# First cross-attention of a Perceiver block: the output product from rounded parts and rests, issued later in the next tile

## The chip, the cores and the metric

The kernel runs on one core of a Trainium2 chip. The metric is the device time of one execution in microseconds. TensorE multiplies, ScalarE and VectorE empty its results from PSUM and do the elementwise work, GpSimd (POOL) clips and does small powers, and the SP queue issues nearly all transfers. Each engine runs its own instruction stream in order; semaphores join the streams.

## The reference, cut to what matters

Six blocks follow one another (cross-attention, self-attention, mixture of experts, cross-attention, self-attention, feed-forward). The change lies in the first, for 16 batches of 64 latents and 256 context rows, width 256, 16 heads of 64 (INNER = 1024):

```python
lat = layernorm(latents, ln_l_w, ln_l_b)
ctx = layernorm(context, ln_c_w, ln_c_b)
q = (lat @ Wq)
k, v = jnp.split(ctx @ Wkv, 2, axis=-1)
attn = jnp.clip(jnp.einsum('bhnd,bhsd->bhns', q, k) * scale, -11.0, 11.0)
attn = jax.nn.softmax(attn, axis=-1)
out = jnp.einsum('bhns,bhsd->bhnd', attn, v)       # heads side by side: 1024 wide
return out @ Wo + bo                               # the output product
```

All is float32, and the result is added to x.

## The kernel before, in words

The stage works in 8 tiles t of 128 latents (two batches, 512 context rows). The key weights are folded into the queries (fill_A), so that scores are taken against the normalised context cT itself. Values (fill_v) and scores use pairs: an operand is rounded to fp32r (hi), the rest is subtracted (lo), and three one-pass products hi hi, hi lo, lo hi stand for one float32 product. The output product alone is a plain float32 one: 8 products of 128x128 by 128x256, which the profile shows as 16 matmul records of line 693.

TensorE's order in a tile t, written out by hand in pe_x0: v2, v3 and scores 0 to 3 in turn, then y(t-1), the output product of the tile before, then the transposes lat(t+1), then v4, scores 4, v5, scores 5, v6, scores 6, v7, values 0, scores 7, then q(t+1), A(t+1), values 1 and v0, v1 of the next tile. All these fills but the scores and values go through a ring of four PSUM banks; the list FILLS fixes the order, and each bank must have been emptied by ScalarE or VectorE before its next use.

Between two tiles the attention result and the normalised context are transposed by a way through DRAM: VectorE writes rows (att, cn), the SP queue stores and reloads them in blocks (turn_rows, turn_att_rows), and VectorE turns 32x32 blocks (turn_context, turn_att). In the last tile TensorE transposes instead (fill_T), in two halves, and two half products y and y2 (fill_y_half, line 701) lie among the first steps of the self-attention stage (pe_self, span 0).

VectorE's order in a tile t: norm(t+2) part 0, turn_context(t+1), turn_att(t-1) twice, v3, cT(t+1), cT_split(t+1), residual(t-1) with its row statistics, norm(t+2) part 1 (two statistics of line 315 and five aggregations of line 320), v5, norm part 2, v7, norm part 3, attend 0, q, A_lower and so on. The rstd for the norm comes from GpSimd (line 327). ScalarE's order: exponentials 0 and 1, v2, exponentials 2 and 3, cT(t+1) (line 754), lat(t+1), v4, exponentials 4 and 5, v6, and so on. cT_split rounds cT (line 899) and subtracts (cT_lo, line 901); it needs both halves of cT, ScalarE's and VectorE's.

Only in tiles with a successor is there a cT, only in those with two a norm. Behind the stage GpSimd adds a bias row to x (line 2111), and the self-attention stage's first steps on VectorE include maximum (lines 1961 to 1967) and rotate (line 1941). The weights w_sq[0] are read from line 1486 on, the expert weights from line 2311 on.

## Time and profile before

| | us |
|---|---|
| median of 3 runs | 1001.73 |
| lowest, highest | 998.05, 1005.35 |
| the profiled execution's own time | 1003.49 |
| its span, first to last instruction | 1001.8 |
| mean granted TensorE clock, of full speed | 0.981 |

The profile is of one execution. Its rows name a line, an engine, an operation, out<-in by the program's names, and shapes in partitions x elements; starts are in us from the span's beginning. A number in brackets behind a row is the engine's idle time before the instruction and what ended it. TensorE's matmuls are pipelined: their length is longer than the distance between their starts, and it is this distance that counts in a stream.

### The profile page before, as it was taken

To read this page: it belongs to the slowest core of one execution; us is meant where nothing else is said; L and a number is where in the kernel's file an instruction comes from. 1 tells how busy PE (TensorE), PEld (TensorE's weight loads), DVE (VectorE), ACT (ScalarE), POOL (GpSimd) and SP (SyncE) were. 2 spreads that over 40 slices of the span, in tenths; PEclk is the share of its full clock that TensorE was granted. 3 is DMA by queue.
4 is the path that set the end of the run, shared out by engine and by line. 5 is a ranking of instruction groups with operands and counts; after the bars stand their busy time and mean duration, and the time that the engine had idled before them with its cause. 6 is when DMAs were issued, how large, how long until landed. Compare 5 with 4: busy or idle time off the path is not lost.

```text
span 1001.8 us, 25859 instructions
## 1 busy us (share of the span) xinstructions
PE 949.6 (95%) x10657; PEld 815.0 (81%) x10657; DVE 613.0 (61%) x1448; ACT 446.1 (45%) x892; POOL 169.3 (17%) x357
## 2 busy tenths in 40 slices
PE   5899999999999989999879999997999999999998
PEld 5788888888888777887669999995888888877887
DVE  5655754654532655667798787776787763554242
ACT  3333332433332476654236666652435343673241
POOL 2312112113112213334320000013113000101000
PEclk9999999999999999999979999997999999999999
DMA  9443142131210292000049999952312002000000
GB/s 321 129 106 74 33 106 68 39 85 42 45 37 7 67 381 98 3 12 24 20 129 332 380 357 358 328 129 57 59 36 45 3 2 76 2 2 1 8 14 22
DMA packets 158611, 101.14 MB, mean 101 GB/s; under 512 B 102104, under 2 KB 148128, under 8 KB 157984
## 3 DMA queue, kind: packets, MB, share of 16 engines
q1 hardware_dynamic: 156960, 95.31, 32.0%
q0 software_dynamic: 1536, 4.20, 1.3%
q8 instruction: 85, 1.39, 0.6%
q14 instruction: 30, 0.25, 0.1%
HBM read 82.96 MB, written 16.52 MB: 99 GB/s over the span
## 4 chain that ended last, share of the span: by engine, by line
PE 82%; DVE 9%; ACT 5%; issue 2%; DMA 1%; POOL 0%; SPq 0%; DVEq 0%; ACTq 0%; POOLq 0%
PE ps L642 9%; PE ps L657 8%; PE ps L2367 8%; PE ps L2380 6%; PE ps L2703 6%; PE ps L674 3%; PE ps L1486 3%; PE ps L1195 3%; PE ps L1583 3%; PE ps L596 2%; PE ps L693 2%; PE ps L626 2%; PE ps L1525 2%; PE ps L1120 2%; PE ps L1130 2%
## 5 line engine op out<-in xcount | busy, mean ns | idle before, releaser
L2367 PE MATMUL ps<-moe_xT,ew 128*128 128x128 f32 x736 | 91.3, 278 | 2.2 <-issue 1.2
L2367 PEld LDWEIGHTS ps<-moe_xT,ew 128*128 128x128 f32 x736 | 87.6, 195 | 3.2 <-DVE moe_xT L2453 1.9
L785 ACT ACTIVATE x0pT<-ps 128x512 f32<-128x512 f32 x64 | 38.2, 598 | 111.1 <-PE ps L657 111.1
L1029 POOL TENSOR_SCALAR x0pT<-x0pT 128x512 f32<-128x512 f32 x64 | 40.6, 635 | 188.3 <-ACT x0pT L785 187.2
L2703 PE MATMUL ps<-f,ffw 128*128 128x512 f32 x256 | 60.7, 398 | 0.8 <-issue 0.6
L2703 PEld LDWEIGHTS ps<-f,ffw 128*128 128x128 f32 x256 | 48.9, 192 | 12.0 <-issue 0.9
L642 PE MATMUL ps<-x0wv_hi,x0cT_hi 128*128 128x512 f32 x128 | 53.6, 418 | 4.2 <-DVE x0A_lo L915 4.2
L2380 PE MATMUL ps<-ew_2hi,eh_hi 128*128 128x256 f32 x184 | 55.4, 301 | 1.7 <-DVE eh_lo L2506 1.3
L2316 DVE TENSOR_TENSOR ew_2lo<-ew,ew_2hi 128x1024 fp32r<-128x1024 f32 x46 | 55.9, 1216 | 0.0
L2563 POOL DMA_INDIRECT yg<-moe_out,slot x16 | 16.3, 1017 | 230.9 <-DMA moe_out<-moe_y 163.5
L915 DVE TENSOR_TENSOR x0A_lo<-ps,x0A_hi 128x512 fp32r<-128x512 f32 x64 | 39.8, 683 | 23.4 <-ACT x0A_hi L776 23.3
L657 PE MATMUL ps<-x0A_hi,x0cT_hi 128*128 128x512 f32 x128 | 51.5, 403 | 2.6 <-ACT x0pT L785 2.6
L921 DVE COPY x0v<-ps 128x512 f32<-128x512 f32 x32 | 22.0, 687 | 50.5 <-PE ps L642 50.5
L2380 PE MATMUL ps<-ew_2hi,eh_lo 128*128 128x256 f32 x184 | 51.7, 281 | 0.0
L2380 PE MATMUL ps<-ew_2lo,eh_hi 128*128 128x256 f32 x184 | 51.6, 281 | 0.0
L642 PE MATMUL ps<-x0wv_hi,x0cT_lo 128*128 128x512 f32 x128 | 50.9, 398 | 0.0
L642 PE MATMUL ps<-x0wv_lo,x0cT_hi 128*128 128x512 f32 x128 | 50.9, 397 | 0.0
L657 PE MATMUL ps<-x0A_lo,x0cT_hi 128*128 128x512 f32 x128 | 50.7, 396 | 0.0
L657 PE MATMUL ps<-x0A_hi,x0cT_lo 128*128 128x512 f32 x128 | 50.2, 392 | 0.0
L389 POOL TENSOR_TENSOR rn_tmp<-rn_cur,eps 128x1 f32<-128x1 f32 x48 | 13.2, 275 | 215.0 <-DVE rn_cur L383 214.3
L2311 ACT ACTIVATE ew_2hi<-ew 128x1024 fp32r<-128x1024 f32 x46 | 49.3, 1072 | 0.0
L2415 ACT ACTIVATE eh<-ps,b1x 128x128 f32<-128x128 f32 x120 | 34.3, 369 | 32.3 <-PE ps L2367 32.3
(336 smaller groups left out, 2416.6 us busy)
## 6 DMA issues: line engine op xcount, KB each, us to landing
ew<-L_ffn_W_dram SPq DMA_DIRECT2D x46, 1024.0 KB, 7.9
x0cin<-ctx_dram SPq DMA_DIRECT2D x8, 512.0 KB, 4.7
x1cin<-ctx_dram SPq DMA_DIRECT2D x64, 64.0 KB, 2.3
x0cn_rows<-x0cn SPq DMA_DIRECT2D x7, 512.0 KB, 2.8
x0cn_blocks<-x0cn_rows SPq DMA_DIRECT2D x56, 64.0 KB, 2.4
x0att_rows<-x0att SPq DMA_DIRECT2D x14, 256.0 KB, 2.5
x0att_blocks<-x0att_rows SPq DMA_DIRECT2D x56, 64.0 KB, 2.7
moe_out<-moe_y SPq DMA_DIRECT2D x23, 128.0 KB, 4.4
```

The costliest lines, as they stand in the source:

```text
L642: last = nc.tensor.matmul(dst, m[:, k, tok * P:tok * P + P], w[:, k, half * 512:half * 512 + 512], start=(k == 0 and n == 0), stop=(k == K ...
L657: last = nc.tensor.matmul(ps[:, S_BANK[u % 2], :], w[:, k, keys], m[:, k, b, pg, :, :, :].rearrange("p a j n -> p (a j n)"), start=(k == 0 ...
L674: last = nc.tensor.matmul(ps[64 * b:64 * b + 64, PV_BANK + par, j * VW:j * VW + VW], g.pT[:, 4 * pg + 2 * b + kt, at_p:at_p + N], g.v[:, 2 ...
L785: nc.scalar.activation(g.pT[:, u, :], ps[:, S_BANK[u % 2], :], ACT.Exp, scale=64.0 ** -0.5).then_inc(C0.exp, 1)
L915: nc.vector.tensor_tensor(g.A_lo[:, kc, :, pg, par, :, :].rearrange("p b j n -> p j b n"), bank_of(t, f"A{gr}{par}").rearrange("p (j b n) ...
L1029: nc.gpsimd.tensor_scalar(g.pT[:, u, :], g.pT[:, u, :], high, low, ALU.min, ALU.max).then_inc(C0.clip, 1)
L2311: nc.scalar.activation(ew2_hi[b % 2][:, sl, :], ew2[b % NW2][:, sl, :], ACT.Copy).then_inc(MO.w_hi, 1)
L2316: nc.vector.tensor_tensor(ew2_lo[b % NW2][:, sl, :], ew2[b % NW2][:, sl, :], ew2_hi[b % 2][:, sl, :].bitcast(F32), ALU.subtract).then_inc( ...
L2367: last = nc.tensor.matmul(ps[:, n % 3, j * BT:j * BT + BT], ew1[b % NW][:, i, f * P:f * P + P], xT[b % 2][:, i, :], start=(i == 0), stop=( ...
L2380: last = nc.tensor.matmul(ps[:, o_bank(b), 0:D], v[:, j * BT:j * BT + BT], w[:, f, :], start=(f == 0 and m == 0), stop=(f == FT - 1 and m ...
L2415: last = nc.scalar.activation(eh[n % 3][:, j * BT:j * BT + BT], ps[:, n % 3, j * BT:j * BT + BT], ACT.Gelu_apprx_tanh, bias=bias)
L2703: last = nc.tensor.matmul(ps[:, 2 + f % 4, :], w[:, k, f * P:f * P + P], src[part][:, k, :], start=(k == 0 and part == 0), stop=(k == ks - ...
```

## The change

The output product is taken as three one-pass products from rounded parts and rests, as the other products are. For this, in tile 0, ScalarE rounds Wo to wo_hi and VectorE subtracts wo_lo, in four pieces each; in tiles 1 to 7 ScalarE rounds attT(t-1) to attT_hi in two pieces behind cT(t+1), and VectorE subtracts attT_lo in two pieces behind norm(t+2) part 1. The product y(t-1) moves behind v5, ahead of scores 5; the residual moves behind v5 on VectorE. In the last tile each half is rounded by ScalarE and its rest taken by VectorE. attT_lo and wo_lo lie over attT and wo. wo_hi lies where w_sq[0] is, so these weights are loaded when the stage is done; attT_hi lies in half of padneg, which is cleared again by a memset on GpSimd then. Counts of semaphores follow (C0.turned, C0.attT, pool_setup), without other effect.

```diff
             attT = sb("x0attT", [P, 8, P])
...
             wo = sb("x0wo", [P, 8, D])
+            wo_lo = nc.alloc_sbuf_tensor_at("x0wo_lo", [P, 8, D], F32R, offset=wo_at)
+            wo_hi = nc.alloc_sbuf_tensor_at("x0wo_hi", [P, 8, D], F32R, offset=w_sq_at)
+            attT_hi = nc.alloc_sbuf_tensor_at("x0attT_hi", [P, 8, P], F32R, offset=padneg_at + B * S)
...
-            FILLS += [(("x0", t - 1), "y")] * (t > 0) + [(("x0", t + 1), "lat")] * nxt
-            FILLS += [(("x0", t), f"v{i}") for i in range(4, 8)]
+            FILLS += [(("x0", t + 1), "lat")] * nxt
+            FILLS += [(("x0", t), f"v{i}") for i in range(4, 6)] + [(("x0", t - 1), "y")] * (t > 0)
+            FILLS += [(("x0", t), f"v{i}") for i in range(6, 8)]
...
+            def out_products(t, what, ks):
+                for k in ks:
+                    for n, (m, w) in enumerate(((g.attT_hi, g.wo_hi), (g.attT_hi, g.wo_lo), (g.attT_lo, g.wo_hi))):
+                        last = nc.tensor.matmul(bank_of(t, what)[:, 0:D], m[:, k, :], w[:, k, :], start=(k == ks[0] and n == 0), stop=(k == ks[-1] and n == 2))
+                last.then_inc(C0.fill, 1)
...
                 if t == 0:
-                    pe.wait_ge(ld["x0o"], 16)
-                pe.wait_ge(C0.attT, 2 * t + 2)
+                    pe.wait_ge(C0.w_lo, KD + 4)
+                pe.wait_ge(C0.attT, 4 * t + 4)
...
-                for k in range(8):
-                    last = nc.tensor.matmul(bank_of(t, "y")[:, 0:D], g.attT[:, k, :], g.wo[:, k, :], start=(k == 0), stop=(k == 7))
-                last.then_inc(C0.fill, 1)
+                out_products(t, "y", range(8))
...
             def fill_y_half(t, what):
                 half = ("y", "y2").index(what)
                 wait_emptied(pe, t, f"T{half}")
...
-                for k in range(4):
-                    last = nc.tensor.matmul(bank_of(t, what)[:, 0:D], g.attT[:, 4 * half + k, :], g.wo[:, 4 * half + k, :], start=(k == 0), stop=(k == 3))
-                last.then_inc(C0.fill, 1)
+                out_products(t, what, range(4 * half, 4 * half + 4))
...
-                if t > 0:
-                    fill_y(t - 1)
                 if nxt:
                     fill_lat(t + 1)
                 for i in range(4, 8):
                     fill_v(t, i)
+                    if i == 5 and t > 0:
+                        fill_y(t - 1)
                     if i == 7:
                         values(t, 0)
                     scores(t, i)
...
-            def attT(t):
-                wait_filled(act, t, "T0")
-                nc.scalar.activation(g.attT[:, 0:4, :], bank_of(t, "T0"), ACT.Copy).then_inc(C0.by_act, 1)
+            def attT_upper(t):
+                act.wait_ge(C0.attT, 4 * t + 2)
+                if t > 0:
+                    wait_filled(act, t - 1, "y")
+                for pg in range(2):
+                    nc.scalar.activation(g.attT_hi[:, 4 * pg:4 * pg + 4, :], g.attT[:, 4 * pg:4 * pg + 4, :], ACT.Copy).then_inc(C0.attT_hi, 1)
+
+            def attT_upper_last(pg):
+                wait_filled(act, T - 1, f"T{pg}")
+                nc.scalar.activation(g.attT_hi[:, 4 * pg:4 * pg + 4, :], bank_of(T - 1, f"T{pg}").rearrange("p (c n) -> p c n", c=4), ACT.Copy).then_inc(C0.attT_hi, 1)
...
+            def wo_upper(i):
+                if i == 0:
+                    act.wait_ge(ld["x0o"], 16)
+                nc.scalar.activation(g.wo_hi[:, 2 * i:2 * i + 2, :], g.wo[:, 2 * i:2 * i + 2, :], ACT.Copy).then_inc(C0.w_hi, 1)
...
@@ -811,13 +833,22 @@
                 exp(t, 3)
                 if nxt:
                     cT(t + 1)
+                if t > 0:
+                    attT_upper(t - 1)
+                if nxt:
                     lat(t + 1)
                 v(t, 4)
                 exp(t, 4)
                 exp(t, 5)
+                if t == 0:
+                    wo_upper(0)
+                    wo_upper(1)
                 v(t, 6)
                 exp(t, 6)
                 exp(t, 7)
+                if t == 0:
+                    wo_upper(2)
+                    wo_upper(3)
                 if nxt:
                     q(t + 1)
                     A_upper(t + 1, 0)
...
-            def attT(t):
-                wait_filled(dve, t, "T1")
-                nc.vector.tensor_copy(g.attT[:, 4:8, :], bank_of(t, "T1")).then_inc(C0.by_dve, 1)
+            def attT_lower(t, pg):
+                dve.wait_ge(C0.attT_hi, 2 * t + pg + 1)
+                half = slice(4 * pg, 4 * pg + 4)
+                nc.vector.tensor_tensor(g.attT_lo[:, half, :], g.attT[:, half, :], g.attT_hi[:, half, :].bitcast(F32), ALU.subtract).then_inc(C0.attT, 1)
+
+            def attT_lower_last(pg):
+                dve.wait_ge(C0.attT_hi, 2 * T - 1 + pg)
+                half = slice(4 * pg, 4 * pg + 4)
+                nc.vector.tensor_tensor(g.attT_lo[:, half, :], bank_of(T - 1, f"T{pg}").rearrange("p (c n) -> p c n", c=4),
+                                        g.attT_hi[:, half, :].bitcast(F32), ALU.subtract).then_inc(C0.by_dve, 1)
+
+            def wo_lower(i):
+                dve.wait_ge(C0.w_hi, KD + i + 1)
+                nc.vector.tensor_tensor(g.wo_lo[:, 2 * i:2 * i + 2, :], g.wo[:, 2 * i:2 * i + 2, :], g.wo_hi[:, 2 * i:2 * i + 2, :].bitcast(F32), ALU.subtract).then_inc(C0.w_lo, 1)
...
                 if nxt:
                     cT(t + 1)
                     cT_split(t + 1)
+                if more:
+                    norm(t + 2, 1)
+                if t > 0:
+                    attT_lower(t - 1, 0)
+                    attT_lower(t - 1, 1)
+                v(t, 5)
                 if t > 0:
                     residual(t - 1)
-                if more:
-                    norm(t + 2, 1)
-                v(t, 5)
                 if more:
                     norm(t + 2, 2)
                 v(t, 7)
                 if more:
                     norm(t + 2, 3)
+                if t == 0:
+                    wo_lower(0)
+                    wo_lower(1)
                 attend(t, 0)
                 if nxt:
                     q(t + 1)
+                if t == 0:
+                    wo_lower(2)
+                    wo_lower(3)
+                if nxt:
                     A_lower(t + 1, 0)
                     A_lower(t + 1, 1)
                     attend(t, 1)
...
-                pe.wait_ge(ld["sq0"], 64)
...
+                if n == LEAD - 2:
+                    pe.wait_ge(ld["sq0"], 64)
...
                 hT(lo)
-                last(T - 1)
+                last(0)
                 lat(lo)
                 qkc(lo)
                 rope(lo)
+                last(1)
                 hT(lo + 1)
                 lat(lo + 1)
                 qkc(lo + 1)
                 hT(lo + 2)
...
                 x0_attend, x0_attT, x0_add_y, x0_residual = last
+                x0_attT(0)
                 rotate(lo)
                 x0_attend(T - 1, 1)
                 v(lo)
                 norm(lo + 1)
-                x0_attT(T - 1)
+                x0_attT(1)
                 norm(lo + 2)
                 x0_add_y(T - 1, "y")
                 maximum(lo)
...
-            for i, w in enumerate(("Wq", "Wk", "Wv", "Wo")):
-                whole(w_sq[0][:, :, i, :], weight("L0_ffn_" + w), ld["sq0"])
...
             sp.wait_ge(C0.x_done, T)
+            for i, w in enumerate(("Wq", "Wk", "Wv", "Wo")):
+                whole(w_sq[0][:, :, i, :], weight("L0_ffn_" + w), ld["sq0"])
             for i, w in enumerate("QKVO"):
                 whole(w_sq[1][:, :, i, :], weight("L1_attn_W_" + w), ld["sq1"])
-            sp.wait_ge(pool_setup, 8)
+            sp.wait_ge(pool_setup, 9)
...
             pool.wait_ge(C0.x_done, T)
+            nc.gpsimd.memset(padneg[:, B // 2:B, :], 0.0).then_inc(pool_setup, 1)
             nc.gpsimd.memset(b2[:, :], 0.0).then_inc(pool_setup, 1)
             nc.gpsimd.memset(minus1[:, :], -1.0).then_inc(pool_setup, 1)
             pool_self(pool, 0)
```

## Rows read from the trace of the kernel before

**Rows 1.** TensorE's waits, 0 to 480 us: who waited <- for whom, sum, times, longest.

```profile
PE ps L642 <- DVE x0A_lo L915: 4.2, 8, 0.6
```

**Rows 2.** Timeline of TensorE, tile 3: start, length, instruction.

```profile
153.72 3.62 PE L693 MATMUL ps<-x0wo,x0attT 128*128 128x256 f32 x16
...
157.18 0.38 PE L583 MATMUL ps<-cst,x0lat 128*128 128x128 f32 x2
...
161.58 0.39 PE L657 MATMUL ps<-x0A_hi,x0cT_hi 128*128 128x512 f32 x1
```

**Rows 3.** Timeline of TensorE, expert stage.

```profile
561.57 0.28 PE L2380 MATMUL ps<-ew_2hi,eh_lo 128*128 128x256 f32 x1
...
562.71 1.95 PE L2367 MATMUL ps<-moe_xT,ew 128*128 128x128 f32 x16
```

**Rows 4.** Timeline of VectorE, tile 3.

```profile
155.98 1.22 DVE L901 TENSOR_TENSOR x0cT_lo<-x0cT,x0cT_hi 128x1024 fp32r<-128x1024 f32 x1
...
160.03 0.45 DVE L320 BATCH_NORM_AGGREGATE ln_mv<-ln_st 128x2 f32<-128x6 f32 x5
161.78 0.69 DVE L921 COPY x0v<-ps 128x512 f32<-128x512 f32 x1 [1.30 <-PE ps L642]
```

**Rows 5.** Timeline of ScalarE, tile 3.

```profile
154.41 0.80 ACT L754 ACTIVATE x0cT<-x0cT,col 128x512 f32<-128x512 f32 x1
```

**Rows 6.** Timeline of VectorE, tile 0.

```profile
45.07 1.23 DVE L901 TENSOR_TENSOR x0cT_lo<-x0cT,x0cT_hi 128x1024 fp32r<-128x1024 f32 x1
...
47.46 0.66 DVE L921 COPY x0v<-ps 128x512 f32<-128x512 f32 x1
```

**Rows 7.** VectorE's subtractions: one line's instructions (ns min/median/max), and a timeline row.

```profile
L2506 DVE TENSOR_TENSOR eh_lo<-eh,eh_hi x46: 691/693/694, 517.2 to 665.4; 128x512 fp32r<-128x512 f32 x46
...
176.24 2.48 DVE L915 TENSOR_TENSOR x0A_lo<-ps,x0A_hi 128x512 fp32r<-128x512 f32 x4 [1.02 <-ACT x0A_hi L776]
```

**Rows 8.** Timeline of TensorE, a first matmul behind a wait.

```profile
105.14 0.50 PE L642 MATMUL ps<-x0wv_hi,x0cT_hi 128*128 128x512 f32 x1 [0.51 <-DVE x0A_lo L915]
```

**Rows 9.** Timelines of TensorE in tile 1 and of VectorE in tiles 1 and 6.

```profile
76.17 3.69 PE L693 MATMUL ps<-x0wo,x0attT 128*128 128x256 f32 x16 [0.20 <-issue]
...
78.14 1.22 DVE L901 TENSOR_TENSOR x0cT_lo<-x0cT,x0cT_hi 128x1024 fp32r<-128x1024 f32 x1
...
272.18 1.22 DVE L901 TENSOR_TENSOR x0cT_lo<-x0cT,x0cT_hi 128x1024 fp32r<-128x1024 f32 x1
```

**Rows 10.** Timeline of VectorE, behind the last product of the stage.

```profile
342.10 0.42 DVE L949 TENSOR_TENSOR x_res<-ps,x_res 128x256 f32<-128x256 f32 x1 [0.29 <-PE ps L701]
```

**Rows 11.** Timeline of VectorE, line 1967 in two places of the next stage.

```profile
346.64 0.65 DVE L1967 SCALAR_TENSOR_TENSOR sa_neg<-sa_max,sa_neg 128x16 bf16<-128x16 f32 x1
...
366.10 0.17 DVE L1967 SCALAR_TENSOR_TENSOR sa_neg<-sa_max,sa_neg 128x16 bf16<-128x16 f32 x1
```

**Rows 12.** Timeline of GpSimd, beside these two, and in tile 3.

```profile
160.84 1.18 POOL L327 TENSOR_TENSOR ln_rs<-ln_ve,neghalf 128x5 f32<-128x5 f32 x1
...
345.17 2.09 POOL L2111 TENSOR_TENSOR x_res<-x_res,rows 128x256 f32<-128x256 f32 x3
...
365.70 0.55 POOL L400 TENSOR_TENSOR rn_tmp<-rn_tmp,neghalf 128x1 f32<-128x1 f32 x1
```

**Rows 13.** TensorE by stretches of tile 0: us, busy (instructions), granted clock, DMA.

```profile
43.50:46.00 2.50, 0.00 (x0) 1.00 0.06 22
47.00:50.00 3.00, 3.00 (x8) 0.50 0.02 5
```

**Rows 14.** Instructions of three lines (ns min/median/max, first and last start us).

```profile
L1486 PE MATMUL ps<-sa_hT,w_sq x128: 275/275/377, 374.1 to 466.0; 128*128 128x128 f32 x128
...
L2311 ACT ACTIVATE ew_2hi<-ew x46: 1052/1072/1079, 373.3 to 664.8; 128x1024 fp32r<-128x1024 f32 x46
...
L2930 POOL MEMSET padneg<- x1: 3520/3520/3520, 1.6 to 1.6; 128x4096 bf16 x1
```

**Rows 15.** The page, part 6: a DMA issue, KB, us to landing.

```profile
ew<-L_ffn_W_dram SPq DMA_DIRECT2D x46, 1024.0 KB, 7.9
```

More of the change, by code:

```diff
@@ L91, in build @@
         maskTi = sb("maskTi", [P, B, 2], I32)
+        padneg_at = at[0]
         padneg = sb("padneg", [P, B, S], BF16)
@@ L173, in build @@
             att = sb("x0att", [P, 8, P])
+            attT_at = at[0]
             attT = sb("x0attT", [P, 8, P])
+            attT_lo = nc.alloc_sbuf_tensor_at("x0attT_lo", [P, 8, P], F32R, offset=attT_at)
             wq = sb("x0wq", [P, KD, INNER])
@@ L179, in build @@
             wv_hi = sb("x0wv_hi", [P, KD, INNER], F32R)
+            wo_at = at[0]
             wo = sb("x0wo", [P, 8, D])
+            wo_lo = nc.alloc_sbuf_tensor_at("x0wo_lo", [P, 8, D], F32R, offset=wo_at)
+            wo_hi = nc.alloc_sbuf_tensor_at("x0wo_hi", [P, 8, D], F32R, offset=w_sq_at)
+            attT_hi = nc.alloc_sbuf_tensor_at("x0attT_hi", [P, 8, P], F32R, offset=padneg_at + B * S)
             ln_st = sb("ln_st", [P, 5, 6])
@@ L484, in build @@
             attT = sem("c0_attT")
+            attT_hi = sem("c0_attT_hi")
             cT_act = sem("c0_cT_act")
-            cT_dve = sem("c0_cT_dve")
             cT_hi = sem("c0_cT_hi")
@@ L546, in build @@
         _more += [(("x1", t), k) for t in range(T) for k in ("q", "k1")]
-        RS = Ring([ps[:, i, :] for i in range(4)], FILLS, ("cT1", "q1", "K1", "K3", "v1", "v3", "v5", "v7", "T1", "rope", "k", "pv", "y", "y2", "router", "rank"),
+        RS = Ring([ps[:, i, :] for i in range(4)], FILLS, ("cT1", "q1", "K1", "K3", "v1", "v3", "v5", "v7", "T0", "T1", "rope", "k", "pv", "y", "y2", "router", "rank"),
                   SA.fill, SA.by_act, SA.by_dve, _more)
@@ L752, in cT @@
                 else:
-                    act.wait_ge(C0.turned, t)
+                    act.wait_ge(C0.turned, 2 * t - 1)
                 nc.scalar.activation(g.cT[:, 0, :], bank_of(t, "cT0") if t == 0 else g.cT[:, 0, :], ACT.Identity,
@@ L827, in act_x0 @@
                     A_upper(t + 1, 3)
-            return attT
+            return attT_upper_last
         def self_tables(dve):
@@ L887, in cT @@
                 else:
-                    dve.wait_ge(C0.turned, t)
+                    dve.wait_ge(C0.turned, 2 * t - 1)
                 nc.vector.tensor_scalar(g.cT[:, 1, :], bank_of(t, "cT1") if t == 0 else g.cT[:, 1, :], vec("ln_c_w", 1), vec("ln_c_b", 1),
-                                        ALU.mult, ALU.add).then_inc(C0.by_dve if t == 0 else C0.cT_dve, 1)
+                                        ALU.mult, ALU.add).then_inc(C0.by_dve if t == 0 else C0.turned, 1)
             def cT_split(t):
@@ L897, in cT_split @@
                     dve.wait_ge(C0.cT_act, t)
-                    dve.wait_ge(C0.cT_dve, t)
+                    dve.wait_ge(C0.turned, 2 * t)
                 nc.vector.tensor_copy(g.cT_hi[t % 2][:, :, :], g.cT[:, :, :]).then_inc(C0.cT_hi, 1)
@@ L1020, in dve_x0 @@
                     self_tables(dve)
-            return attend, attT, add_y, residual
+            return attend, attT_lower_last, add_y, residual
         def pool_x0(pool):
@@ L1860, in act_self @@
             else:
-                act.wait_ge(pool_setup, 9)
+                act.wait_ge(pool_setup, 10)
                 x1_neg, x1_attT, x1_exps = last
@@ L2496, in gates @@
                 dve.wait_ge(MO.route, ROUTE[T, "w_pick"])
-                dve.wait_ge(pool_setup, 10)
+                dve.wait_ge(pool_setup, 11)
                 nc.vector.tensor_tensor(gate[:, :, 0:E], pslot[:, :, 0, :], pslot[:, :, 1, :], ALU.add).then_inc(MO.gate, 1)
@@ L2812, in turn_rows @@
                 if t > 1:
-                    sp.wait_ge(C0.turned, t - 1)
+                    sp.wait_ge(C0.turned, 2 * t - 3)
                 blocks = cn_dram.rearrange("(m j) (k q i) -> q k j m i", j=32, k=KD, i=32)
@@ L2824, in turn_att_rows @@
                 if t > 0:
-                    sp.wait_ge(C0.attT, n - 1)
+                    sp.wait_ge(C0.attT, 4 * t + pg - 3)
                 blocks = att_dram[pg].rearrange("(m j) (c q i) -> q j c m i", j=32, c=4, i=32)
```

## Prediction

> **What bounds the kernel now.** The page shows TensorE busy nearly all the time, but a share over stages with different limits only says where to look. The change touches the first cross-attention, tiles 0 to 7, from the start to about 342 us, so the first view that counts is TensorE's waits up to 480 us. There the only wait that comes back once in every tile is on the VectorE subtraction of line 915 at the end of a tile, 0.5 us each [rows 1]. In this stage, then, TensorE's instruction stream is the time: what is shortened there is gained, and a new wait there is lost. The second view is the timeline of tile 3 on three engines [rows 2, 4, 5]; tiles 2 to 5 repeat it every 38.7 us with the same offsets. The reader is to see there when VectorE is through with cT_lo, and what its queue holds next.
>
> **The products themselves.** For tiles 0 to 6 the product is issued in the middle of the next tile: 16 matmul records on line 693 (8 products, two passes each), seven times. In tile 3 they take 157.18 - 153.72 = 3.46 us, 0.216 us per record [rows 2]. The new form, three products of 128x256 with fp32r operands, is run by the expert stage: ten follow one another in 562.71 - 561.57 = 1.14 us, 0.114 us each [rows 3]. 24 of them are 2.74 us. So TensorE saves 0.72 us in each of tiles 1 to 7, and for each half in the last tile 8 x 0.216 - 12 x 0.114 = 0.36 us.
>
> **Whether the operands are there in time.** The products now wait for two subtractions (attT_lo) that VectorE issues after cT(t+1), cT_split(t+1) and part 1 of norm(t+2). Take tile 3, and call 153.72 T0, the end of its fourth scores, where the old product began.
>
> TensorE's side: from T0 it now runs lat, v4, scores 4 and v5. Before, these took 161.58 - 157.18 = 4.40 us behind the product [rows 2]. It would reach the new product at 158.12.
>
> VectorE's side: cT_split must wait for ScalarE's cT, which starts behind the fourth exponential at 154.41 and lasts 0.80 [rows 5]. That start depends on the fourth scores alone, so the moved product does not shift it; cT_lo starts at 155.98 as before [rows 4]. From there to the first instruction behind part 1 of the norm is 2.39 us: tile 0 runs just this sequence without a wait, 45.07 to 47.46 [rows 6]. The two subtractions are the form of line 2506, 0.69 us each; four like them on line 915 last 2.48 us together, so they follow at 0.60 us [rows 7]. The second ends at 155.98 + 2.39 + 0.60 + 0.69 = 159.66, and TensorE starts some 0.04 later (my allowance for the semaphore), at 159.70. ScalarE's two roundings sit behind cT, end at about 155.1 + 2 x 0.6 = 156.3, and do not decide.
>
> So TensorE waits 159.70 - 158.12 = 1.58 us; a restart costs 0.11 more, because the first matmul behind a wait lasts 0.50 us [rows 8] where the others of its line last 0.39 or 0.40. Net for tiles 2 to 5: 1.69 + 2.74 - 3.46 = **+0.97 us each, +3.9**. The wait that pays for it is VectorE's order, not its load: before v5 it idled for 1.3 us [rows 4], but that gap lies behind norm part 1, and the subtractions come when TensorE should have them already.
>
> The other tiles. Tile 1: the old product waited 0.20 us and started at 76.17, cT_lo starts at 78.14 [rows 9]. T0 is 75.97, TensorE is there at 80.37, the subtractions at 78.14 + 2.39 + 1.29 + 0.04 = 81.86; 1.49 + 0.11 + 2.74 - 3.66 = **+0.7**. Tile 6 has no norm behind cT_split: the first subtraction can start 1.14 us behind cT_lo (0.08 before it ends), 272.18 + 1.14 + 1.29 + 0.04 = 274.65 [rows 9], against T0 = 272.18 - 2.26 = 269.92 (the offset of tile 3) and 269.92 + 4.40 = 274.32; 0.44 + 2.74 - 3.46 = **-0.3**. Tile 7 has neither cT nor norm, so VectorE is free early: **-0.7**. Tile 0 has no output product. It gets eight extra instructions for splitting the weights (some 0.6 us each, as above) on ScalarE and VectorE; they fall into gaps that the tile has in both queues, and the waits behind them (q, the A products) can slip by 0.2 us at most: I take 0.
>
> **What is queued behind the new waits.** On TensorE scores 5 and all later work of the tile slip with it (that is the sum above). On VectorE v5 stands behind the subtractions and the residual behind v5; the residual now waits for the product (T0 + 8.9), and norm part 2 behind it comes some 2 us later than before. Its readers are the SP queue's row turn and the lat transposes of the next tile, both more than ten us away. On ScalarE lat, v4 and exponential 4 slip by 1.2 us; scores 6, which need that exponential, now stand over 8 us behind T0. The DMAs of the attention turn wait for the same transposes as before.
>
> **The last tile.** Each half of the attention is now rounded by ScalarE and then subtracted by VectorE, where two copies ran side by side. The first half is early in both queues. For the second, ScalarE's rounding is behind rope and VectorE's subtraction behind norm: some 0.6 us later, while its product comes several us later. The path then runs from the second product to VectorE's addition at 342.10, which had waited 0.29 us for it [rows 10]. Both halves gain: 2 x 0.36, **-0.65** taken.
>
> **Moved weights and memset.** Four transfers of w_sq[0] leave the opening and are issued when the stage ends (342 us). Their first reader, line 1486, runs at 374.1 [rows 14]: 30 us of cover. A transfer four times as large lands in 7.9 us [rows 15], and that would be the price without cover. They also put 1 MB before the expert weights, which line 2311 first reads at 373.3 [rows 14]: a delay of under 8 us in 30. Both 0. What the opening gains from moving 1 MB less I take as 0 too: the row turn that tile 0 waits for is released by VectorE's norm, not by the transfers before it. The memset of half of padneg is half of 3.52 us [rows 14], on GpSimd behind the stage. It delays the three additions of line 2111 that start at 345.17 [rows 12] and slow VectorE's small instructions on the path: line 1967 takes 0.65 us beside them and 0.17 elsewhere [rows 11], and line 1965 before it likewise. If the memset does not disturb VectorE, 0.9 us is gained there; if it does, or if the additions hit other instructions of the path, 0. Middle: **-0.45**.
>
> **Sum.** 3.9 + 0.7 - 0.3 - 0.7 - 0.65 - 0.45 = +2.5 us. The profiled execution has a span of 1001.8 us and took 1003.49; the median of the runs is 1001.73, so the same step on the median gives **1004.2 us**. The runs lie 998.05 to 1005.35 apart; a change under 1% (10 us) counts as none here.
>
> **Rivals.**
> *The operands are in time (gain kept).* Then seven tiles give 0.72 each: -5.0 - 0.65 - 0.45 = -6.1, 995.6 us. For it: 1.6 us is a small margin built from three durations. Against it: each of them repeats, and VectorE takes its queue in order. 12%.
>
> *GpSimd holds VectorE up.* Behind norm part 1 GpSimd computes the reciprocal root, 1.18 us [rows 12], starting 0.36 us behind the aggregation's end (160.48, [rows 4]), just when the two subtractions run. The first of them starts before it. If the second has to wait for it to end, that subtraction starts 0.36 + 1.18 us behind the aggregation instead of 0.5: 1.0 us later, in tiles 1 to 5: +5, 1009.2 us. For it: line 1967, with two operands in SBUF, took 0.65 beside line 2111. Against: the same line took 0.17 us at 366.10, in the middle of the power of line 400 (365.70, 0.55 us) [rows 11, 12]. 10%. The Trainium skill (SBUF — State Buffer, Who interferes with whom) says that a VectorE instruction with two SBUF inputs and a GpSimd instruction that reads SBUF exclude each other for the whole instruction; by that rule this case happens whenever the power starts first, and the trace agrees for line 2111 but not for the power.
>
> *The clock falls (the slower side).* In tile 0 TensorE stood for 2.57 us (idle from 43.5 to 46) and was then granted half its clock, 1.2 of 2.4 GHz, from 47 to 50 us [rows 13]: 1.5 us lost. A wait of 1.6 us in the middle of dense work is shorter than that, and the 0.5 us waits do nothing. If it happens in one tile it costs 1.5, in five 7.5: 1011.7 us; slower by over 1% only with all five. 9% for that.
>
> **Chances and range.** The forecast (VectorE's order costs about what is saved) 60%; gain kept 12%; GpSimd 10%; clock in all five tiles 9%; the last 9% is for small things elsewhere, within some us. Leaving out the first rival and the last gives 997 to 1010. Faster by over 1% 3% (even the full gain is 6 us), slower by over 1% 9%, within 88%.
>
> **What would show it.** TensorE's product in tiles 2 to 5 some 6 us behind the fourth exponential's release, with about 1.6 us idle before it, released by VectorE's subtraction; in tile 6 under 0.5, in tile 7 none. 24 records of 0.114 us pace. A tile period of 39.7 instead of 38.7 us. The second half's product 0.36 us shorter. I am wrong if the product starts without a wait in tiles 2 to 5, if the two subtractions take longer than 0.7 us, or if the clock row shows half speed between 80 and 300 us.

## The result and the profile after

| | before | after |
|---|---|---|
| median, six runs each | 1002.37 us | 1015.52 us |
| lowest, highest | 998.05, 1005.35 | 1007.22, 1019.57 |
| the profiled execution's span | 1001.8 us | 1012.4 us |
| its mean granted TensorE clock | 0.981 | 0.973 |

The ratio is 1.0099, with a 95% interval of 1.0065 to 1.0132; the medians of the table lie further apart, by 1.3%. The forecast was 1004.2 us. So the kernel became slower, as forecast, but by 13 us instead of 2.5, and outside the range of 997 to 1010. The table hints that two things are in this number: work, and a clock that was granted differently in the two profiles.

**The stage.** TensorE's waits from 0 to 480 us, after (who waited <- for whom: sum, times, longest):

```profile
PE ps L698 <- DVE x0attT_lo L975: 5.8, 5, 1.4
PE ps L650 <- DVE x0A_lo L946: 4.2, 8, 0.6
...
PE ps L698 <- issue: 1.8, 1, 1.8
```

The second row is the old one [rows 1]. The first is new, and it is the wait of the forecast: the product on the subtraction of VectorE. Tile 3, TensorE, then VectorE, ScalarE and GpSimd (start, length):

```profile
159.31 0.39 PE L650 MATMUL ps<-x0wv_hi,x0cT_lo 128*128 128x512 f32 x1
...
161.11 0.38 PE L698 MATMUL ps<-x0wo_hi,x0attT_hi 128*128 128x256 f32 x1 [1.41 <-DVE x0attT_lo L975]
...
163.92 0.28 PE L698 MATMUL ps<-x0wo_hi,x0attT_lo 128*128 128x256 f32 x1
...
164.03 0.40 PE L665 MATMUL ps<-x0A_hi,x0cT_hi 128*128 128x512 f32 x1
```

```profile
157.39 1.23 DVE L932 TENSOR_TENSOR x0cT_lo<-x0cT,x0cT_hi 128x1024 fp32r<-128x1024 f32 x1
...
159.43 0.45 DVE L327 BATCH_NORM_AGGREGATE ln_mv<-ln_st 128x2 f32<-128x6 f32 x5
159.79 1.26 DVE L975 TENSOR_TENSOR x0attT_lo<-x0attT,x0attT_hi 128x512 fp32r<-128x512 f32 x2
160.97 0.68 DVE L952 COPY x0v<-ps 128x512 f32<-128x512 f32 x1
164.23 0.42 DVE L991 TENSOR_TENSOR x_res<-ps,x_res 128x256 f32<-128x256 f32 x1 [2.58 <-PE ps L698]
```

```profile
155.82 0.81 ACT L764 ACTIVATE x0cT<-x0cT,col 128x512 f32<-128x512 f32 x1
156.53 1.14 ACT L802 ACTIVATE x0attT_hi<-x0attT 128x512 fp32r<-128x512 f32 x2
```

```profile
159.96 0.55 POOL L332 TENSOR_TENSOR ln_ve<-ln_mv,eps 128x5 f32<-128x5 f32 x1 [3.33 <-DVE ln_mv L327]
160.58 1.51 POOL L334 TENSOR_TENSOR ln_rs<-ln_ve,neghalf 128x5 f32<-128x5 f32 x1
```

The subtractions start 2.40 us behind cT_lo, as tile 0 had shown (2.39, [rows 6]), although attT_hi had been ready since 157.67. TensorE's last row of v5 starts at 159.31; in a stream the next would start 0.23 later, at 159.54. The product starts at 161.11: 1.57 us late. It lasts to 164.03, 2.92 us. 1.57 + 2.92 - 3.46 = +1.03 us for this tile (3.46 is what the old product took). From one cT_lo to the next, tiles 2 to 6, it is 39.79 us, where it was 38.73 (155.98 and 272.18 of [rows 4] and [rows 9] are three periods apart): +1.06. The clock stayed whole there (us, TensorE busy, granted clock, DMA share, GB/s):

```profile
80.00:300.00 220.00, 210.05 (x1980) 1.00 0.26 59
```

**Beyond the stage.** Two places in the order of time. The first is line 1507 (1455 before), the transposes that open the self-attention; the second is line 1667 (1615 before), which places tokens for the experts. One line's instructions of each kernel (ns min/median/max, first and last start); before:

```profile
L1455 PE MATMUL ps<-cst,h x48: 272/273/329, 325.6 to 880.9; 128*128 128x128 f32 x48
...
L1615 PE MATMUL ps<-hot,u x32: 379/379/795, 491.0 to 509.3; 128*128 128x256 f32 x32
```

After:

```profile
L1507 PE MATMUL ps<-cst,h x48: 272/273/330, 329.4 to 893.1; 128*128 128x128 f32 x48
...
L1667 PE MATMUL ps<-hot,u x32: 379/380/792, 500.3 to 520.1; 128*128 128x256 f32 x32
```

The first place comes 3.8 us later; the placing starts 9.3 us later and ends 10.8 us later. Of the change, only the two halves of the last product, the memset and the wait for the moved weights lie between the two. The rows of stretches show what else differs, before:

```profile
476.00:480.00 4.00, 4.00 (x52) 0.63 0.00 0
...
484.00:488.00 4.00, 3.60 (x55) 1.00 0.01 4
...
492.00:496.00 4.00, 2.98 (x17) 1.00 0.00 0
...
508.00:512.00 4.00, 3.10 (x9) 0.50 0.21 70
```

After:

```profile
480.00:484.00 4.00, 2.86 (x52) 1.00 0.02 4
484.00:488.00 4.00, 3.34 (x41) 0.80 0.00 0
488.00:492.00 4.00, 4.00 (x47) 0.50 0.02 4
...
500.00:504.00 4.00, 3.53 (x10) 0.50 0.00 0
504.00:508.00 4.00, 4.00 (x17) 0.64 0.00 0
```

In the routing steps, behind a stretch in which TensorE was idle for 1.1 of 4 us, this execution was granted 0.50, that is 1.2 of 2.4 GHz, for some 20 us on end. The execution of before had such stretches too, but shorter ones: from 460 to 524 us they add up to 14 us, and to 27 us after. Idle time alone does not tell them apart, since before idled 1.0 of 4 us from 492 and kept the full clock for the next 8 us. The question for the runs was whether the longer stretch belongs to the change.

### The profile page after: what moved, and what is told of

It reads as the page before. It is cut to its first block, busy times and chain, and to the rows that moved or that the text cites. A ratio compares the mean times of both kernels' runs of the same rounds, so it can differ in the third digit from the quotient of the medians.

```text
span 1012.4 us, 26032 instructions
## 1 busy us (share of the span) xinstructions
PE 953.5 (94%) x10721; PEld 819.0 (81%) x10721; DVE 626.7 (62%) x1467; ACT 453.2 (45%) x911; POOL 173.1 (17%) x358
## 4 chain that ended last, share of the span: by engine, by line
PE 80%; DVE 10%; ACT 5%; issue 3%; DMA 1%; POOL 0%; SPq 0%; DVEq 0%; ACTq 0%; POOLq 0%
PE ps L665 8%; PE ps L2422 7%; PE ps L650 7%; PE ps L2435 6%; PE ps L2758 6%; PE ps L1538 3%; PE ps L682 3%; PE ps L1247 3%; PE ps L1635 3%; PE ps L1577 2%; PE ps L604 2%; PE ps L698 2%; PE ps L634 2%; PE ps L1172 2%; PE ps L1182 2%
## 5 line engine op out<-in xcount | busy, mean ns | idle before, releaser
L1329 ACT ACTIVATE x1pT<-ps,maskT 128x1024 f32<-128x1024 f32 x32 | 33.9, 1111 | 21.5 <-PE ps L1230 21.5
```

The lines of the kernel that those rows point to most:

```text
L1329: nc.scalar.activation(g.pT[:, b, kt, :, :, :].rearrange("p r f n -> p r (f n)"), Q1[:, :, kt * S:kt * S + S], ACT.Exp, bias=maskT[:, 2 * ...
```

## The experiments

Each run lists its time and its mean granted clock, and all kernels are measured beside the one before. One straight line through the 258 executions of nine kernels that have both, with a constant of its own for each kernel, gives 7.5 us for 0.01 of mean clock and leaves 1.2 us of scatter. The column "at equal clock" is the difference of a kernel's constant to that of before (with its standard error). The four longest executions of before (1015 to 1022 us, clock 0.965 to 0.968) are in the line and the table but not in the ratios below; without them the line gives 7.3 us for 0.01, and the column moves by 0.2 at most. All ratios below lie within 1% of 1. "Period" is from one cT_lo to the next in tiles 3 to 5; tile 2 has the same, save in the orders with early rounding and the new place, where it is 37.6.

| kernel (executions) | median us | mean clock | at equal clock | period |
|---|---|---|---|---|
| before (112) | 1003.6 | 0.9802 | 0 | 38.73 |
| after (42) | 1009.2 | 0.9782 | +4.0 ± 0.2 | 39.79 |
| subtractions ahead of norm (12) | 1002.6 | 0.9799 | -2.7 ± 0.4 | 38.55 |
| early rounding (24) | 1000.6 | 0.9781 | -5.7 ± 0.3 | 38.11 |
| weights and memset only (12) | 1005.3 | 0.9803 | +0.7 ± 0.4 | 38.76 |
| place only, plain product (24) | 1006.8 | 0.9767 | -0.8 ± 0.3 | 38.73 |
| early rounding, old place (8) | 1011.9 | 0.9779 | +5.0 ± 0.4 | 39.43 |
| more filler (12) | 1002.7 | 0.9798 | -2.1 ± 0.4 | 38.11 |
| memset later (12) | 1000.6 | 0.9769 | -6.1 ± 0.4 | 38.12 |

**The changed kernel again**, three times, each beside runs of the kernel before.

> The changed kernel again, beside the others. Theory S (the stage is 4 us longer since TensorE waits for attT_lo, and the rest of the 10 us is half clock in the routing steps at 480 to 520 us, a matter of the single execution): median between 1006 and 1016, the single runs ordered by their granted clock: those at 0.980 near 1007, those at 0.968 near 1017. Theory M (the moved weights and memset cost time behind the stage): the same, but also runs at 0.980 above 1012.

> The changed kernel a third time, on whichever chip it comes. Theory C (the time beyond the stage's 4 us is half clock that single executions draw, in the changed kernel as in the one before): time plus the clock's share as in the second set, about 988 us at full clock against 985 for the kernel before, and granted clocks as those of the kernel before in this set. Theory D (the change itself makes the clock fall more often): mean granted clock lower by 0.005 or more than the kernel before's in this set, median above 1012.

> The changed kernel once more, to weigh its clocks. So far 7 of its 29 executions had a mean granted clock of 0.973 or less (1013 us and more), 8 of 65 of the kernel before; the means are 0.978 and 0.981. Theory C (single executions draw the half-clock stretches, whatever the kernel): 1 or 2 of 12 at 0.973 or less, a mean clock within 0.001 of that of the kernel before in the same set, ratio about 1.004 (the 4.1 us of the stage and its tail). Theory D (the change shifts the work so that the clock falls more often): 3 or more of 12, a mean clock lower by 0.003 or more, ratio about 1.007.

Measured: 1007.98, 1009.50 and 1008.55 us; ratios 1.0037 [1.0009, 1.0066], 1.0066 [1.0040, 1.0093] and 1.0063 [1.0034, 1.0092]. The period was 39.79 or 39.80 us in every profile. No execution with a clock of 0.980 or more lay above 1010.3 us, so nothing speaks for theory M. The last of these profiles has the mean clock of the kernel before, 0.981, and there next to nothing is lost beyond the stage:

```profile
L1507 PE MATMUL ps<-cst,h x48: 272/273/330, 329.9 to 887.4; 128*128 128x128 f32 x48
...
L1667 PE MATMUL ps<-hot,u x32: 379/379/796, 495.1 to 513.2; 128*128 128x256 f32 x32
```

+4.3 us at the first place and +4.1 at the second. The same program, line for line, lies 5.2 us earlier at the second place than in the first profile of after, where the clock was 0.973. In the four profiles of this one program the way from the first place to the second took 165.1, 165.2, 167.3 and 170.9 us, and TensorE was at half clock for 0, 0, 7 and 16 us of it; before took 165.4 with 3.4. So the 13 us of the first set are not what the change costs: its six executions had a mean clock of 0.9730, and 0.0072 less than before is 5.4 us by the line. 4.0 + 5.4 = 9.4 is the difference of the means (1014.1 and, over all executions of before, 1004.8 us). The rest of the 13 us is chance of the small sets: the six of before had a mean of 1002.2, 2.6 us under that of all, and their clocks, but for the profiled one, are not on record. In the third set 3 of 12 executions were at 0.973 or less and the mean clock was 0.9784 beside 0.9798: between the two expectations, and neither is shown by it. The second set, with a mean clock of 0.9785 beside 0.9802 and a median of 1009.50, shows neither a fall of 0.005 nor the 1012 us of theory D.

**Where the subtractions stand on VectorE.** The subtractions are put ahead of norm part 1, and nothing else.

```diff
-                if more:
-                    norm(t + 2, 1)
                 if t > 0:
                     attT_lower(t - 1, 0)
                     attT_lower(t - 1, 1)
+                if more:
+                    norm(t + 2, 1)
```

> VectorE takes the two subtractions attT_lo ahead of part 1 of norm(t+2) instead of behind it. Theory S: the wait before the product falls from 1.2 to at most 0.2 us in tiles 1 to 5, 5 x 1.25 = 6 us less than the changed kernel at the same clock, so 1.5 to 2 us below the kernel before. Rival W (another wait takes its place, for instance scores 5 on exponential 3 or v6 on the lat copies, or the stall goes to norm part 2): less than 2 us less. Theory M: no difference in the part behind the stage.

Measured: 1002.63 us, ratio 0.9984 [0.9961, 1.0007]. The waits of TensorE, 0 to 345 us:

```profile
PE ps L698 <- DVE x0attT_lo L975: 0.9, 5, 0.2
```

The wait of 1.4 us is 0.2 now, and the period falls from 39.79 to 38.55. At equal clock this one move is worth 4.0 + 2.7 = 6.7 us, where 6 was expected. The wait was VectorE's order, as argued, and norm part 1 was what stood in it.

**The operands fully in time.** ScalarE rounds behind exponential 2, ahead of exponential 3 and cT; VectorE subtracts between cT and cT_split. The product stays in its new place.

```diff
                 exp(t, 2)
+                if t > 0:
+                    attT_upper(t - 1)
                 exp(t, 3)
...
                     cT(t + 1)
-                    cT_split(t + 1)
-                if more:
-                    norm(t + 2, 1)
                 if t > 0:
                     attT_lower(t - 1, 0)
                     attT_lower(t - 1, 1)
+                if nxt:
+                    cT_split(t + 1)
+                if more:
+                    norm(t + 2, 1)
```

> ScalarE rounds attT behind exponential 2, VectorE subtracts between cT and cT_split, in a gap of 1.6 us; the rest as in the changed kernel. Theory S: no wait of TensorE before the product in any tile, tile period 38.0 us, 7 x 0.7 us less than the kernel before in the stage, 996 to 997 at equal clock. Rival W: period stays at 38.7 or more.

> The version with early splits and the new place again: period 38.1 us, 979 us at full clock by the reckoning time x granted clock, against 985 for the kernel before; median 2 to 6 us below the kernel before in this set, by how the clocks fall.

Measured: 1000.99 and 1000.31 us, ratios 0.9966 [0.9939, 0.9993] and 0.9974 [0.9943, 1.0005]. Tile 3, ScalarE, VectorE and TensorE of the first:

```profile
149.46 1.14 ACT L802 ACTIVATE x0attT_hi<-x0attT 128x512 fp32r<-128x512 f32 x2
```

```profile
151.43 1.29 DVE L974 TENSOR_TENSOR x0attT_lo<-x0attT,x0attT_hi 128x512 fp32r<-128x512 f32 x2
```

```profile
155.74 0.39 PE L650 MATMUL ps<-x0wv_hi,x0cT_lo 128*128 128x512 f32 x1
155.97 0.28 PE L698 MATMUL ps<-x0wo_hi,x0attT_hi 128*128 128x256 f32 x1
```

The subtractions are done some 3 us before the product starts. It follows v5 at 0.23 us, without a wait, and the period is 38.11: 0.62 below before, where 0.72 was the saving of the products alone. This is the first rival of the forecast made true by another order. It gave 995.6 us there; the kernel has 1000.6 as a median at its clocks, and 5.7 us less than before at equal clock, beside the 6.1 of the rival's sum. At equal clock it is faster than both kernels; of the two ratios to the kernel before, one has 1 inside its interval.

**Early rounding, product in the old place.** The residual goes back ahead of norm part 1 with it.

```diff
...
+                if t > 0:
+                    fill_y(t - 1)
                 if nxt:
                     fill_lat(t + 1)
                 for i in range(4, 8):
                     fill_v(t, i)
-                    if i == 5 and t > 0:
-                        fill_y(t - 1)
...
                     cT_split(t + 1)
+                if t > 0:
+                    residual(t - 1)
                 if more:
                     norm(t + 2, 1)
                 v(t, 5)
-                if t > 0:
-                    residual(t - 1)
```

> Rounded operands split early (ScalarE behind exponential 2, VectorE between cT and cT_split), but the product in its old place right behind scores 3. The subtractions end some 1.2 us behind the end of scores 3. Theory S: TensorE waits 1.2 to 1.4 us in tiles 2 to 6, period 39.4 us, 3 to 5 us slower than before at equal clock: the new place is needed for the new form. If the period is 38.1 as with the new place, the place was not needed.

Measured: 1011.89 us, ratio 1.0088 [1.0057, 1.0120], and TensorE's waits, 0 to 345 us:

```profile
PE ps L697 <- DVE x0attT_lo L973: 6.5, 6, 1.6
...
PE ps L697 <- issue: 2.9, 1, 2.9
```

The period of 39.43 and +5.0 us at equal clock are what was expected (39.4, 3 to 5). Here the early subtractions still come too late by up to 1.6 us, since they stand behind cT. The product needs both the later place and the earlier operands; the change has the place alone.

**The place alone, with the plain product**, twice. The product and the residual move as in the change; the product keeps its 16 records.

> The kernel before with the plain float32 product issued behind v5 and the residual behind v5 on VectorE, nothing else. Theory S: no wait of TensorE before the product, period 38.7 us, same time as before within 1 us: the place costs nothing by itself. Rival (the place costs: scores 5, v6 or norm part 2 come late): 39 us or more per tile.

> The plain float32 product in the new place, once more, for its clocks: the first time its twelve executions had a mean granted clock of 0.976 beside 0.980 for the kernel before, five of them at 0.973 or less, although TensorE waits nowhere more than before. If a work order with the product in the new place draws the half-clock stretches more often (theory D): again a mean clock lower by 0.003 or more than before's in the same set, and a ratio of 1.003 or more in spite of 1.7 us less at full clock. If those were draws (theory C): a mean clock within 0.0015 of before's, and a ratio of 0.997 to 1.001.

Measured: 1006.52 and 1006.87 us, ratios 1.0039 [1.0007, 1.0071] and 1.0002 [0.9969, 1.0036]. The period is that of before, and at equal clock it is 0.8 us less: tile 1 is 0.7 shorter, where the old product started late [rows 9]. So the move costs nothing in work. But its mean clocks were 0.9763 and 0.9771, beside 0.9802 and 0.9796 for the kernel before in the same sets. The second is 0.0025 less, under the 0.003 that one theory asked and over the 0.0015 of the other; its ratio of 1.0002 is where theory C had it (0.997 to 1.001), and D had asked for 1.003 or more. Its profile had 0.970, and the half clock stands in the same place as in the first profile of after:

```profile
480.00:484.00 4.00, 2.20 (x31) 1.00 0.00 0
484.00:488.00 4.00, 4.00 (x43) 0.69 0.02 4
...
500.00:504.00 4.00, 3.53 (x9) 0.50 0.00 0
504.00:508.00 4.00, 4.00 (x21) 0.75 0.00 0
```

**Moved weights and memset alone**, in the kernel before.

```diff
-            for i, w in enumerate(("Wq", "Wk", "Wv", "Wo")):
-                whole(w_sq[0][:, :, i, :], weight("L0_ffn_" + w), ld["sq0"])
...
             sp.wait_ge(C0.x_done, T)
+            for i, w in enumerate(("Wq", "Wk", "Wv", "Wo")):
+                whole(w_sq[0][:, :, i, :], weight("L0_ffn_" + w), ld["sq0"])
...
             pool.wait_ge(C0.x_done, T)
+            nc.gpsimd.memset(padneg[:, B // 2:B, :], 0.0).then_inc(pool_setup, 1)
```

> The kernel before with one part of the change: the four w_sq[0] transfers issued behind the stage, and half of padneg cleared once more by GpSimd there. Nothing is left out of the computation. Theory S: same as before within 1 us at equal clock, and its runs spread over the granted clock like those of before. Theory M: 3 to 6 us slower, with half clock in the routing steps or a wait behind 342 us.

Measured: 1005.28 us, ratio 1.0019 [0.9998, 1.0040], +0.7 ± 0.4 us at equal clock. In its profile the fourth pair of line 1455's transposes starts 22.89 us behind the first; before it was 22.04. That 0.85 is the memset, as the next run shows; what the moved weights cost, if anything, is below the 0.4 us of uncertainty.

**The memset later.** The early rounding, with the memset behind the first four additions of the bias row.

```diff
             pool.wait_ge(C0.x_done, T)
-            nc.gpsimd.memset(padneg[:, B // 2:B, :], 0.0).then_inc(pool_setup, 1)
...
+                if span == 0 and n == lo + 1:
+                    nc.gpsimd.memset(padneg[:, B // 2:B, :], 0.0).then_inc(pool_setup, 1)
                 if n + 3 < hi and is_mla(n + 3):
```

> The early rounding (label e2_split_early), with the memset of half of padneg on GpSimd moved behind the first four additions of the bias row, away from VectorE's maximum and norm. If the memset holds VectorE up there, as the profile of the change seems to say: VectorE's tensor_scalar of the maximum 0.62 us instead of 0.86 and the norm's application 0.40 instead of 0.88, the first hT transposes of the next stage 0.5 to 0.8 us earlier against the end of the first cross-attention, and a median 0.5 to 1 us below e2's 1000.6. If these instructions are slow because of something else: the same durations, no gain.

The first steps of the self-attention on GpSimd and VectorE, after:

```profile
348.02 1.80 POOL L2989 MEMSET padneg<- 128x2048 bf16 x1
...
350.08 2.82 POOL L2166 TENSOR_TENSOR x_res<-x_res,rows 128x256 f32<-128x256 f32 x4
```

```profile
349.29 0.86 DVE L2019 TENSOR_SCALAR sa_neg<-sa_max 128x16 bf16<-128x16 f32 x1
350.18 0.65 DVE L2021 SCALAR_TENSOR_TENSOR sa_neg<-sa_max,sa_neg 128x16 bf16<-128x16 f32 x1
350.75 0.87 DVE L418 TENSOR_SCALAR h<-x_res,rn_mean,rn_rs 128x256 f32<-128x256 f32 x1
```

And with the memset later, GpSimd and VectorE:

```profile
339.14 2.09 POOL L2166 TENSOR_TENSOR x_res<-x_res,rows 128x256 f32<-128x256 f32 x3
```

```profile
340.09 0.49 DVE L2019 TENSOR_SCALAR sa_neg<-sa_max 128x16 bf16<-128x16 f32 x1
340.62 0.65 DVE L2021 SCALAR_TENSOR_TENSOR sa_neg<-sa_max,sa_neg 128x16 bf16<-128x16 f32 x1
341.19 0.40 DVE L418 TENSOR_SCALAR h<-x_res,rn_mean,rn_rs 128x256 f32<-128x256 f32 x1
```

Line 2019 (349.29 to 350.15) starts while the memset runs (to 349.82) and takes 0.37 us more than beside the additions. Line 418 does not meet the memset at all: it meets the additions, which the memset has pushed onto it; with the memset later they end at 341.2, as line 418 starts, and it takes 0.40 instead of 0.87. That is 0.84 together, and the fourth pair of transposes of line 1507 starts 21.43 us behind the first instead of 22.28. The median, 1000.56 us, ratio 0.9965 [0.9936, 0.9994], can't be told from the 1000.6 without this edit; at equal clock it is 0.4 ± 0.5 less. So the gain is shown in the trace, not in the time. Line 2021 takes 0.65 with and without the memset: that one is due to the additions of line 2166 [rows 11, 12].

**More filler.** The routing steps contain products that only keep TensorE busy. The early rounding, with some eight more of them.

```diff
-                        keep_clock(RS.bank(n - 1, "T"), 3 if n == hi - 2 else 2)
+                        keep_clock(RS.bank(n - 1, "T"), 5 if n == hi - 2 else 4)
...
-                    keep_clock(RS.bank(n - 1, "T"), 2)
+                    keep_clock(RS.bank(n - 1, "T"), 4)
```

> The early rounding (label e2_split_early), with more of the matmuls that the kernel issues only to keep TensorE busy, in the last steps of the self-attention before the experts: 5, 4 and 4 instead of 3, 2 and 2 at each of their places, some 8 more of 0.43 us. If the half-clock stretches between 475 and 515 us come from TensorE's idle gaps there: no stretch of more than 3.4 us in this place in the profile, a mean clock of 0.982 or more, a median of 996 to 999 us beside e2's 1000.6. The rival, that the gaps there don't decide or that the filler holds up real products: 1 to 4 us more than e2, the clock as before.

Measured: 1002.66 us, ratio 0.9979 [0.9951, 1.0006]. The profile still has half clock in that place:

```profile
476.00:480.00 4.00, 2.19 (x9) 0.90 0.00 0
480.00:484.00 4.00, 4.00 (x40) 0.50 0.00 0
484.00:488.00 4.00, 4.00 (x50) 0.75 0.10 35
```

None of its 12 executions was at 0.973 or less, where 11 of the 36 of the same kernel without the filler (memset later among them) were; so the filler may well keep the longest stretches away. But its mean clock is only 0.0017 above that of the early rounding, some 1.3 us by the line, and at equal clock it costs 3.6 us more. The rival is what was measured: the filler costs more than it brings.

**Where the clock goes.** Of the fourteen profiled executions four have a mean clock of 0.970 to 0.973 (after, place only, early rounding, memset later), and in these TensorE ran at half clock for 27 to 38 of the 64 us from 460 to 524 us. The other ten, clock 0.978 to 0.985, have 7 to 17 us there. The kernel before draws this too: 17 of 112 executions at 0.973 or less, against 10 of 42 of after. The mean clocks differ by 0.0021 ± 0.0010, which is 1.6 us. For the four orders with the product in the new place and no filler (after, early rounding, place only, memset later, 102 executions) it is 0.0026 ± 0.0007. But these four are picked with the result known: "subtractions ahead of norm" has the product in the new place too and shows next to no difference (0.0003), while "early rounding, old place" has it in the old one and lies 0.0023 lower (8 executions, ± 0.0016). That the new place makes the draw likelier is thus possible, not shown, and no row tells by what it would: with the place alone moved, the program from the stage's end to the place where the clock falls is that of before.

## The forecast, step by step

**TensorE reaches the product at T0 + 4.40: right.** In tile 3 after, T0 is 157.39 - 2.26 = 155.13 and v5 is through at 159.54, T0 + 4.41.

**VectorE's order sets the start: right.** Forecast was T0 + 5.98, measured 161.11 - 155.13 = 5.98. The two subtractions lasted 1.26 us together (1.29 forecast), ScalarE's rounding ended long before, and the undoing of this one order took the wait away.

**The products: a little more.** The pace is 0.117 us a record in place of the 0.114 of [rows 3], so 24 take 2.81 us, and 2.92 with the restart, where 2.85 was forecast. A tile came to +1.06 instead of +0.97: four tiles +4.2 instead of +3.9. (The forecast calls the two records of one float32 product its passes. A record took 0.216 us, near twice the 0.117 of a one-pass product of the same shape, so what a record holds is not shown; the sum does not need it.)

**Tiles 1, 6 and 7: right.** The first rows of the product in tiles 1, 6 and 7:

```profile
81.57 0.36 PE L698 MATMUL ps<-x0wo_hi,x0attT_hi 128*128 128x256 f32 x1 [1.81 <-issue]
...
279.26 0.39 PE L698 MATMUL ps<-x0wo_hi,x0attT_hi 128*128 128x256 f32 x1 [0.18 <-DVE x0attT_lo L975]
...
317.24 0.28 PE L698 MATMUL ps<-x0wo_hi,x0attT_hi 128*128 128x256 f32 x1
```

Tile 1 came to 39.80 - 39.10 = +0.7 (+0.7). Tile 6 waits 0.18 us, tile 7 not at all, and the two together gain 0.8 (1.0). The weight split in tile 0 is hidden: its period is 33.37 beside 33.07, but the kernels with the place alone moved, which have no such split, have 33.32 and 33.16.

**The last tile's halves: right.** With the memset out of the way the fourth pair of transposes stands 0.61 us closer to the first than before (21.43 and 22.04); 0.65 was forecast.

**The memset: the term that was mis-sized, in sign too.** -0.45 was taken, between -0.9 and 0. I had named both ways in which it went, the memset beside VectorE and the additions on other instructions of the path, and gave them 0. They cost 0.84 us in the early rounding and 0.85 in the kernel before. Zero was no bound for a delay: line 1965 and the norm's application, the next two instructions of the path, should have been priced with the additions or the memset upon them. Together with the halves the tail came to +0.2 or +0.3, not to -1.1.

**Sum in the stage.** +2.5 was forecast. At equal clock the runs give +4.0 ± 0.2: 1.3 of the tail, 0.3 of the four tiles and 0.2 of tiles 6 and 7 are what it was short of, 1.8 for a difference of 1.5. That alone would have been 1005.7 us, inside the range.

**The clock outside the stage: the step that was missing.** I asked what the clock does in tiles 1 to 5, where the granted clock is 1.00 in the profile after, so the third rival did not happen. The sum has no term for the clock behind the stage: it takes the span's 0.981 as fixed. It is a draw of each execution, between 0.970 and 0.988 for the kernel before alone (its four longest left out), and 0.01 of it is 7.5 us. The first set of the changed kernel drew 0.973, worth 5.4 us. Three runs that lay 7 us apart had this in them, and the range made no room for it: with it, an end of some 1015 would have been due, and 1015.52 would still have lain at its edge. Which way a set of six falls could not be forecast; that the change itself shifts the draw is open, as said above. That the sign of the forecast came true rests on the mechanism: the same sign stands at equal clock.

**The GpSimd rival: the mechanism was there, the other way round.** VectorE came first, and GpSimd was held. Line 332 took 0.55 us beside the subtractions and line 334 took 1.51, where line 327 of before took 1.18 [rows 12] and the line ahead of it 0.20:

```profile
160.57 0.20 POOL L325 TENSOR_TENSOR ln_ve<-ln_mv,eps 128x5 f32<-128x5 f32 x1 [5.36 <-DVE ln_mv L320]
```

The result is wanted only by norm parts later, so this cost nothing. The Trainium skill (SBUF — State Buffer, Who interferes with whom) has it that issue order decides which of the two is blocked; the trace agrees.

## What to carry to other kernels

When an operation gets a new operand that another engine must prepare, find that engine's place in its own order first: here 1.4 us of wait or more in five tiles ate a saving of some 0.65 in seven, and moving two instructions ahead of a part that nobody was waiting for turned +4.0 us into -2.7. Every instruction added to GpSimd is priced against what VectorE does beside it, with a loss as one end. And before a difference of some us is explained, lay the granted clock of each execution beside its time; a single profile, or six runs, can carry 5 us of clock.

## Hardware behaviour that was not expected

- VectorE's tensor_scalar is held up by GpSimd although it has one operand in SBUF: one of 128x256 took 0.87 us beside additions and 0.40 without them; one of 128x16 took 0.86 when it began in a memset and 0.49 beside additions. The Trainium skill (SBUF — State Buffer, Who interferes with whom) says that tensor_scalar can enter a mode that takes the ports shared with GpSimd, and then blocks or is blocked; the trace agrees for both. It does not agree everywhere: in the kernel before, the same 128x16 form (line 1965) took 0.17 us at 365.88, in the middle of the power of line 400 [rows 12], and 0.62 beside the additions at 345.98.
- Operations with two SBUF operands on VectorE lengthened GpSimd's own small ones, from 1.18 to 1.51 us and from 0.20 to 0.55 us.
- With the same program, the kernel before, the mean granted clock of single executions ran from 0.970 to 0.988, and the times with it from 1012.6 to 1000.6 us (its four longest left out). Nearly all of the difference between the profiles at 0.970 to 0.973 and the others lay in one place, the routing steps between 460 and 524 us, where TensorE has gaps of some 1 to 2 us in 4.
